# A routed expert stage whose first tiles get fixed places: transformer block on one Trainium2 core

## The reference

```
x = x + xattn(layernorm(x), ctx)      # one head, softmax over 4096 keys, then a projection
x = x + attn(layernorm(x))            # 16 heads of 16, windows of 64, causal over two windows
x = x + moe(layernorm(x))             # 8 experts, inner width 1024, top 2

logits = x_flat @ gate_w.T
top_v, top_i = top_k(logits, 2);  probs = softmax(top_v)
combine = einsum('tk,tke->et', probs, one_hot(top_i, 8))
for each expert e:  out += combine[e][:, None] * ((silu(x_flat @ wg[e].T) * (x_flat @ wu[e].T)) @ wd[e].T)
```

## Time and profile before

| what | value |
|---|---|
| median of 3 runs | 635.89 us |
| profiled execution | 635.36 us, span 633.6 us |
| PE busy | 598.0 us (94%) |
| DVE busy | 457.9 us (72%) |
| ACT busy | 336.0 us (53%) |
| POOL busy | 255.7 us (40%) |
| mean DMA rate over the span | 241 GB/s |

### The profile page before, as it was taken

How to read it: one execution, slowest core, us unless ns; L and a number is a source line. 1 busy time by engine, 2 the same in 40 slices (tenths; PEclk the granted TensorE clock), 3 DMA queues, 4 the chain that set the end, 5 groups by cost and what they waited for, 6 DMA issues and landing times. The chain is left out here.

```text
span 633.6 us, 10820 instructions
## 1 busy us (share of the span) xinstructions
PE 598.0 (94%) x4008; PEld 514.0 (81%) x4008; DVE 457.9 (72%) x803; ACT 336.0 (53%) x603; POOL 255.7 (40%) x313
## 2 busy tenths in 40 slices
PE   8999999899999999999999858999999999999993
PEld 7889988898889988996667646788888888888882
DVE  4867588767886697769888957776767767677750
ACT  4447522762367334554776652656565655657540
POOL 3317820784058433684454613123132332323312
PEclk9999999999999999999999977999999999999998
DMA  8988887899869647861000346999999999999933
GB/s 286 321 305 234 259 324 207 224 278 315 279 190 281 196 134 183 235 172 43 1 3 1 135 141 233 377 333 336 350 323 360 325 343 339 340 353 335 358 100 83
DMA packets 66035, 152.62 MB, mean 241 GB/s; under 512 B 7504, under 2 KB 47952, under 8 KB 55088
## 3 DMA queue, kind: packets, MB, share of 16 engines
q1 hardware_dynamic: 61568, 145.91, 68.8%
q0 software_dynamic: 4416, 6.03, 5.5%
HBM read 121.52 MB, written 31.46 MB: 241 GB/s over the span
## 5 line engine op out<-in xcount | busy, mean ns | idle before, releaser
L630 ACT ACTIVATE wide_high<-region_a 128x1024 fp32r<-128x1024 f32 (+1 forms) x108 | 105.6, 994 | 101.5 <-PE psum L1599 89.6
L1078 DVE TENSOR_TENSOR wide_low<-region_a,wide_high 128x1024 fp32r<-128x1024 f32 x92 | 112.2, 1221 | 64.0 <-ACT wide_high L630 64.0
L566 POOL TENSOR_TENSOR wide_low<-region_a,wide_high 128x512 fp32r<-128x512 f32 x64 | 82.4, 1290 | 18.4 <-ACT wide_high L630 14.4
L1616 PE MATMUL psum<-region_a,region_w 128*128 128x256 f32 x368 | 83.2, 379 | 0.3 <-ACT region_w L630 0.3
L1379 PE MATMUL psum<-turned_high,wide_low 128*128 128x256 f32 x256 | 79.6, 311 | 2.4 <-DVE turned_low L989 1.5
L1599 PE MATMUL psum<-wide_high,turned_low 128*128 128x512 f32 x184 | 77.9, 424 | 1.5 <-issue 0.8
L1616 PEld LDWEIGHTS psum<-region_a,region_w 128*128 128x128 f32 x368 | 69.6, 190 | 10.7 <-issue 0.5
L1379 PE MATMUL psum<-turned_high,wide_high 128*128 128x256 f32 x256 | 72.4, 283 | 0.0
L1379 PE MATMUL psum<-turned_low,wide_high 128*128 128x256 f32 x256 | 72.2, 282 | 0.0
L1599 PE MATMUL psum<-wide_high,turned_high 128*128 128x512 f32 x184 | 72.1, 392 | 0.0
L1599 PE MATMUL psum<-wide_low,turned_high 128*128 128x512 f32 x184 | 71.9, 391 | 0.0
(11 more groups left out here) (201 smaller groups left out, 1205.4 us busy)
## 6 DMA issues: line engine op xcount, KB each, us to landing
region_a<-turned_up SPq DMA_DIRECT2D x23, 2048.0 KB, 9.9
region_a<-turned_down SPq DMA_DIRECT2D x23, 1024.0 KB, 7.5
region_a<-ctx_dram SPq DMA_DIRECT2D x16, 1024.0 KB, 8.9
turned_up<-region_w SPq DMA_DIRECT2D x64, 256.0 KB, 4.2
region_w<-L_ffn_wg_dram SPq DMA_DIRECT2D x16, 512.0 KB, 6.4
region_w<-L_ffn_wu_dram SPq DMA_DIRECT2D x16, 512.0 KB, 6.1
region_w<-L_ffn_wd_dram SPq DMA_DIRECT2D x16, 512.0 KB, 5.8
turned_down<-region_w SPq DMA_DIRECT2D x32, 256.0 KB, 4.2
```

Of the source, the lines that this page charges most:

```text
L566: nc.gpsimd.tensor_tensor(val_lo[:, g % 4], ctx_sb[n][:, g * PAIR:(g + 1) * PAIR, :], val_hi[:, g % 4].bitcast(F32), ALU.subtract).then_in ...
L630: return nc.scalar.activation(dst, src, ACT.Copy)
L1078: nc.vector.tensor_tensor(w_lo[:, k % RING], group_of(k), w_hi[:, k % RING].bitcast(F32), ALU.subtract).then_inc(low_ready, 1)
L1616: last = nc.tensor.matmul(bank[6][:, 0:D], hidT[n][:, ic * P:(ic + 1) * P], rows, start=ic == 0, stop=ic == IC - 1)
```

## The change

It does the following.

- Expert e gets tile e as its first tile, whatever the counts. Only the tiles beyond the first of an expert (`MORE` = 15) are placed by the counts, from tile 8 on. `owner` covers only these; it is computed on VectorE in the iteration of tile 1, and the weights of tiles 0 to 7 are loaded without it.
- SyncE's order becomes: up 1, down 0, the store that starts the sums, down 1, and then for j from 2: up j, down j. The waits inside `load_up` and `load_down` stay as they are.
- The one-hots of rows are made by 16 `tensor_scalar` operations, one per pick group, on a bf16 input; those of tiles are bf16 too, with the picks innermost. TensorE starts with each pick as it is ready, with two matmuls for each in place of one.
- GpSimd makes one gather of spare rows before it waits for the tokens.
- Two warm-up matmuls in place of four after the tokens' matmuls.
- In `tile_up` the parts that read the high half of the rows come first, and the wait for the low half moves behind them; VectorE splits the rows of tile 1 ahead of a low part.

The diff, cut to its core:

```
-WARM_ROUTED = [4, 1, 1]
+WARM_ROUTED = [2, 1, 1]
...
             def expert_of(rows, j):
-                if j == 0:
-                    return rows[0:1]
-                return rows[bass.ds(sp.value_load(owner[0:1, j:j + 1], min_val=0, max_val=E - 1), 1), :, :]
+                if j < E:
+                    return rows[j:j + 1]
+                sp.wait_ge(owner_ready, 1)
+                return rows[bass.ds(sp.value_load(owner[0:1, j - E:j - E + 1], min_val=0, max_val=E - 1), 1), :, :]
...
+            load_up(1)
             load_down(0)
-            sp.wait_ge(owner_ready, 1)
-            load_up(1)
             sp.wait_ge(xg_loaded[0], 16)
             sp.wait_ge(heads_added, len(LAST_ROWS))
             sp.dma_start(sum_dram[0:TOK, :].rearrange("(t p) d -> p t d", p=P), xr).then_inc(sums_begun, 16)
+            load_down(1)
             for j in range(2, SLOT_TILES):
                 load_up(j)
-                load_down(j - 1)
-            load_down(SLOT_TILES - 1)
+                load_down(j)
...
+            pool.indirect_dma_start(out=xg[AHEAD - 1], out_offset=None, in_=x3_dram,
+                                    in_offset=bass.IndirectOffsetOnAxis(ap=spare_i[:, 0:1], axis=0)).then_inc(spare_gathered, 16)
+            pool.wait_ge(spare_gathered, 16)
             pool.wait_ge(tokens_ready, 1)
...
-            then(nc.vector.tensor_tensor(started, need[:, :].rearrange("p (a f) -> p a f", a=1).broadcast_to([P, E, E]), lower_i, ALU.mult))
-            then(nc.vector.tensor_reduce(first[:, :], started, axis=X_AXIS, op=ALU.add))
-            then(nc.vector.tensor_tensor(begun, ...))
-                nc.vector.tensor_reduce(owner[:, :], begun, axis=X_AXIS, op=ALU.add).then_inc(owner_ready, 1)
+            nc.vector.tensor_tensor(level, ranks, over_t(first_slot[:, :]), ALU.add)
+            then(nc.vector.tensor_reduce(need[:, 0:E], started, axis=X_AXIS, op=ALU.add))
+            then(nc.vector.tensor_tensor(weighed, need[:, :].rearrange("p (a f) -> p a f", a=1).broadcast_to([P, E, E + 1]), lower_i, ALU.mult))
+            then(nc.vector.tensor_reduce(more_at[:, :], weighed, axis=X_AXIS, op=ALU.add))
+            then(nc.vector.scalar_tensor_tensor(out=past_first, in0=ranks, scalar=float(P), in1=over_t(more_at[:, :]), op0=ALU.is_ge, op1=ALU.mult))
+            then(nc.vector.tensor_tensor(level, level, past_first, ALU.add))
...
+            def row_placed(i):
+                return nc.vector.tensor_scalar(place_row[:, i, :], row_numbers[:, :], row_of_pick[:, i:i + 1], None, ALU.is_equal)
+            is_tile = place_tile[:, 0]
+            last = nc.vector.tensor_tensor(is_tile, each_tile, per_pick(tile_of_pick[:, :]), ALU.is_equal)
+            for i in range(2):
+                row_placed(i).then_inc(places_ready, 1)
+            then(last)
+            nc.vector.tensor_scalar(place_tile[:, 1], is_tile, row_number[:, :], None, ALU.mult)
+            nc.vector.tensor_tensor(place_tile[:, 2], is_tile, per_pick(tile_of_token[:, :]), ALU.mult).then_inc(tiles_placed, 1)
+            for i in range(2, PICKS):
+                row_placed(i).then_inc(places_ready, 1)
...
                     if g == 0:
-                        pe.wait_ge(xgT_ready, j + 1)
+                        pe.wait_ge(xgT_high, j + 1)
...
-                        parts = ((xgT_lo, w_hi), (xgT_hi, w_lo), (xgT_hi, w_hi))
+                        parts = ((xgT_hi, w_lo), (xgT_hi, w_hi), (xgT_lo, w_hi))
```

More of the change, by code:

```diff
@@ L218, in perceiver @@
         steps = sb("steps", E)
[L219 to L223, removed]
+        need = sb("more_tiles", E + 1)
+        more_at = sb("more_tiles_at", E)
+        owner = sb("owner", MORE, I32)
+        begun = sb("begun", MORE * (E - 1))[:, :].rearrange("p (j e) -> p j e", j=MORE)
         psum = stack.enter_context(nc.psum_tensor("psum", [P, 8 * BANK], F32))
@@ L1135, in _ @@
                 then(nc.vector.tensor_reduce(slot[:, :], picked.rearrange("p n t e -> p (n t) e"), axis=X_AXIS, op=ALU.add))
[L1136 to L1140, removed]
-            nc.vector.tensor_tensor(ways[:, :, 0], way_base[:, :], row_i[:, :], ALU.subtract)
@@ L1143, in _ @@
-            then(nc.vector.tensor_tensor(is_tile, tileno[:, :].rearrange("p (a j) -> p a j", a=1).broadcast_to([P, PICKS, SLOT_TILES]),
-                                         per_pick(tile_i[:, :], SLOT_TILES), ALU.is_equal))
-            for v in range(2):
-                nc.vector.tensor_tensor(place_tile[:, :, v, :], is_tile, ways[:, :, v:v + 1].broadcast_to([P, PICKS, SLOT_TILES]), ALU.mult)
-            for n in range(TOPK):
-                half = slice(n * TILES, (n + 1) * TILES)
-                nc.vector.tensor_tensor(place_row[:, half, :], row_numbers[:, :].rearrange("p (a r) -> p a r", a=1).broadcast_to([P, TILES, P]),
-                                        per_pick(row_i[:, half], P), ALU.is_equal).then_inc(places_ready, 1)
+            then(nc.vector.tensor_scalar(row_i[:, :], slot[:, :], P - 1, None, ALU.bitwise_and))
@@ L1157, in _ @@
             found = bank[6][:, 0:2 * SLOT_TILES].rearrange("p (v j) -> p v j", v=2)
-            then(nc.vector.tensor_scalar(beside[:, :], found[:, 0], spare_row[:, :], None, ALU.add))
+            then(nc.vector.tensor_scalar(beside[:, :], found[:, 0], minus_spare[:, :], spare_row[:, :], ALU.mult, ALU.add))
             nc.vector.tensor_tensor(token[:, :], beside[:, :], found[:, 1], ALU.add).then_inc(tokens_ready, 1)
@@ L1164, in _ @@
             for v in range(PARTS):
-                last = nc.vector.tensor_tensor(place_prob[:, :, v, :], is_tile, per_pick(prob_parts[:, v], SLOT_TILES), ALU.mult)
+                last = nc.vector.tensor_tensor(place_prob[:, v], is_tile, per_pick(prob_parts[:, v]), ALU.mult)
             last.then_inc(probs_placed, 1)
@@ L1196, in _ @@
                 low(4 * j + 3)
-                if j + 1 < SLOT_TILES:
+                if j == 0:
+                    tile_xgT(1, 1)
+                    low(4)
+                elif j + 1 < SLOT_TILES:
                     low(4 * j + 4)
@@ L1207, in _ @@
                     tile_y(j - 1, 1 - n)
+                if j == 1:
+                    then(nc.vector.tensor_tensor(begun, more_start, more_at[:, 1:E].rearrange("p (a e) -> p a e", a=1).broadcast_to([P, MORE, E - 1]),
+                                                 ALU.is_ge))
+                    with nc.allow_low_precision(reason="a count up to 7"):
+                        nc.vector.tensor_reduce(owner[:, :], begun, axis=X_AXIS, op=ALU.add).then_inc(owner_ready, 1)
             tile_y(SLOT_TILES - 1, 0)
@@ L1545, in _ @@
             last.then_inc(ranks_done, 1)
-            for n in range(TOPK):
-                pe.wait_ge(places_ready, n + 1)
-                for i in range(n * TILES, (n + 1) * TILES):
-                    last = nc.tensor.matmul(bank[6][:, 0:2 * SLOT_TILES], place_row[:, i, :], place_tile[:, i].rearrange("p v j -> p (v j)"),
-                                            start=i == 0, stop=i == PICKS - 1)
+            pe.wait_ge(tiles_placed, 1)
+            place_parts = place_tile.rearrange("p v j i -> p (v j) i")
+            for i in range(PICKS):
+                pe.wait_ge(places_ready, i + 1)
+                nc.tensor.matmul(bank[6][:, 0:2 * SLOT_TILES], place_row[:, i, :], place_parts[:, 0:2 * SLOT_TILES, i], start=i == 0, stop=False)
+                last = nc.tensor.matmul(bank[6][:, SLOT_TILES:2 * SLOT_TILES], place_row[:, i, :], place_parts[:, 2 * SLOT_TILES:, i],
+                                        start=False, stop=i == PICKS - 1)
             last.then_inc(inverse_done, 1)
@@ L1561, in _ @@
             for i in range(PICKS):
-                last = nc.tensor.matmul(bank[6][:, 0:PARTS * SLOT_TILES], place_row[:, i, :], place_prob[:, i].rearrange("p v j -> p (v j)"),
+                last = nc.tensor.matmul(bank[6][:, 0:PARTS * SLOT_TILES], place_row[:, i, :], place_prob.rearrange("p v j i -> p (v j) i")[:, :, i],
                                         start=i == 0, stop=i == PICKS - 1)
```

82 lines of the change are left out of this document (50 added, 32 removed).

## The result

The changed kernel takes 824.64 us (median, 823.19 to 826.46) beside 635.9 us before: ratio 1.298, 95% interval 1.295 to 1.301. The forecast was 829 us, range 752 to 852. The profiled execution has a span of 821.7 us.

The account below looks back on a forecast made before the run. TensorE and the DMA engines were both full, TensorE ending last. The sum was 635.4 us, plus 195 for the rings, plus 0.5 for iteration 1, minus 2 for routing: 829 us, range 752 to 852.

Parts of the forecast that it names:

- The ring: SyncE's up j+1 issue stands behind down j's wait for down matmuls: period 19.8 us for 10.03, 20 times, 195 us.
- The signs: Traces: down and up issued in pairs, ScalarE waiting 10 us for `turned_up`, TensorE pausing near 7 us, clock at 0.5.
- rival B: The ring holds but the clock does not fall or returns at once: 776 us, or 750 with faster transfer; chance 0.24.
- The transfer: From down issue to landing of up behind it: 10.2 us for 3 MB plus indirect traffic, 11.5 us taken.
- From landing to issue: Ring steps: 0.96 us high part, 0.74 us hidden copy, 3.69 us down matmuls, 0.18 us to next issue; 5.6 us.
- The clock: TensorE's 7.1 us pause drops the clock, so down matmuls start at half rate: 2.7 us more in each of 20 rings.
- rival A: The ring with a falling clock in TensorE's pause: 829 us, own range 787 to 857; likeliest, chance 0.60.
- The register load: SyncE's value load of owner, 1.1 us, from tile 8 on: lies beside the 5 us down transfer, worth 0.
- Iteration 1: Down 1 now lies ahead of up 2 on SyncE, which goes out near 394: 0.5 us lost, between 0 and 2.6.
- fixed places: Up 1 no longer waits 7.5 us for `owner`, but nothing waited for that: worth 0.
- setup: The added setup iotas on GpSimd cost nothing, as it idles 8.68 us behind its setup.
- Routing: Routing chain, one-hots, first gather, fewer warm-up matmuls and part order: -2.3 us, rounded to -2, bounds -4 and +1.5.

Follow-up runs that it names:

- experiment 1: The changed kernel with SyncE's old order in the loop (up j, down j-1), nothing else undone: 635.0 us, ratio 0.9994 to the kernel before.
- experiment 2: The kernel before with only SyncE's new order (down 1 ahead of the loop, then up j, down j): 832.99 us, ratio 1.309.
- 4: The changed kernel with ScalarE copying the hidden rows of tile j-1 before it waits for the up weights of tile j+1: 702.42 us, ratio 1.106.
- 5: The changed kernel with down weights from tile 2 on issued by GpSimd, with the same wait, and SyncE issuing only up weights: 646.27 us, ratio 1.019.
- experiment 3: The changed kernel with 14 matmuls on zeros in the pause ahead of the down matmuls of tiles 1 to 20: 775.18 us, ratio 1.219.
- experiment 10: The changed kernel with SyncE's old order in the loop and without the gather of spare rows: 633.98 us, ratio 0.9971 to the kernel before.

## Why the prediction was right, point by point

**The ring.** Right in place and in cause. Experiments 1 and 2 show that the order is both necessary and sufficient; 4 and 5 open the ring at ScalarE and at SyncE and take 122 and 178 us off. The loss is 20 rings at 19.51 us, 20 x (19.51 - 10.03) = 190 us, and the kernel is 189 us slower; 195 were forecast for the rings. The signs came too, in part with other sizes: ScalarE waits 7.65 us for `turned_up` in the ring shown where 10 were expected, and the pair with the register load is 1.13 us apart where 1.5 were. The range begins at 752 us where the sum for rival B's low end gives 750; nothing hangs on it.

**The transfer.** It took 11.71 us for 11.5, and 11.24 us in the rings that the forecast describes, those without a register load. Its two parts hold there: the pair without indirect traffic lands after 10.15 us for 10.2, and that traffic is worth 1.09 us where 1.5 was its price and 1.3 was taken. What this does not show is that each single megabyte costs 2.6 us. The price that the Trainium skill gives (DMA: Bandwidth & Descriptors, Anatomy of one DMA) stands in a section on transfers that GpSimd issues, and these are SyncE's; the 9.2 us worked out from it for the pair lie under the 10.15 us measured.

**From landing to issue.** It is 1.68 or 1.69 us in 20 of 20 rings for the forecast 0.96 + 0.74, and 0.03 us (first rings) or 0.18 us (later ones) at the end for 0.18.

**The clock.** It fell in the pause, as rival A had it and against rival B. The term was 5.98 - 3.69 = 2.3 us a ring for 2.7, and experiment 3 bought it back: 49 us. The two times behind it were read from other places and did not carry over: in the ring shown the clock fell 2.6 us into the pause, not 4.6, and was back 3.2 us after the down matmuls had begun, not 5.4. The Trainium skill (TensorE: Matmul & The Clock Gate, HAM oscillation) says of such a DMA-waiting loop that it loses the clock in each step; the trace agrees, with down matmuls of 5.09 to 6.70 us in all 20 rings for 3.61 at full clock.

**The register load.** This was wrong: it was costed at nothing, beside the 5 us of the down transfer. The rings with it are 19.78 us long, those without 18.71, and 0.62 of the 1.07 us are landing time; experiment 2 has the longer ones from the start. Here luck has a part in the total. The rings without the load came out 1.09 us under the 19.8 forecast (0.26 in the transfer, 0.6 in the clock, 0.15 at the end), and the load, in 15 of 20 rings, put 0.80 us of the mean back.

**Iteration 1, fixed places, setup.** The kernel of experiment 1 still has the early up 1, so that costs nothing, as forecast; the gain of early loading is none either, by 635.0 us. The half microsecond put on iteration 1 does not show: down 2 goes out 16.88 us after the first expert matmul in the changed kernel, and after 17.61 us before.

**Routing.** This term was too large: -2 us were forecast, and the two measurements of the old order with the new routing have -0.4 and -0.9 us, with intervals from +0.6 to -1.7. From the first reduction to the tokens it is 11.12 us before and 10.63 us in the changed kernel, 0.5 us less for the 0.6 forecast, so this part was right. The 0.7 us for the gather of spare rows did not come (experiment 10), and the first matmuls at the low clock take back some of what the earlier start gives. The error of 1 to 1.5 us is small beside the 189.

## What to carry to other kernels

On an engine that issues in order, a wait belongs to everything behind it: before two issues are swapped, ask of each which event it waits for and which other transfer then inherits that wait. A ring is priced by walking it once, from an event back to itself, with one row per step; if it is longer than the busy time of the full engine, the difference times the number of turns is the loss, and the pause that it makes can bring a clock term on top. To price a part of a transfer, leave out whole rows and look at the packets: an edit that halves each row changes the rate along with the size. And compare the start of a stage between two traces from the stage's own first instruction; two profiles of one kernel differed here by 1.5 us before the stage began.

## What the runs showed of the hardware that was not expected

- Halving each row of the down transfer (1 MB to 0.5 MB in as many packets) brought the landing of the up transfer behind it forward by 0.3 to 0.4 us, where 1 MB and 2 MB alone differ by 2.6 us: in the third microsecond the DMA engines were 90% busy and moved 259 GB/s for 420.
- A register load of 1.1 us between the two issues lengthened the ring by 1.07 us, though the first transfer takes 4.8 us to land.
- In the ring shown above the clock fell 2.6 us into the pause and was back 3.2 us after the down matmuls had begun; after the routing of the kernel before it took 5.4 us.
- With 14 matmuls on zeros in each pause the clock stayed at 1.00 from 400 to 600 us, and the kernel was 6% faster than without them; in the one ring where 1.86 us of pause were left behind them the down matmuls took 5.41 us for 3.72.
